# Thresholds of a top-64 attention by a sorting network in two of eight row blocks

## The reference, cut to what matters

```python
dots = jnp.einsum('hg,bgij->bhij', W_pre_th, dots)
dots = jnp.where(causal[None, None], mask_value, dots)
top = jax.lax.top_k(dots, TOPK)[0]          # TOPK = 64
vk = top[..., -1:]                          # the 64th largest: the row's threshold
dots = jnp.where(dots < vk, mask_value, dots)
attn = jax.nn.softmax(dots, axis=-1)
attn = jnp.einsum('hg,bgij->bhij', W_post_th, attn)
```

## Time and profile before

| what | value |
|---|---|
| three runs | 1380.62, 1382.27 (median), 1384.27 us |
| the profiled execution | 1383.52 us |
| its span | 1381.7 us, 18391 instructions |
| DVE busy | 1012.6 us, 73% of the span |
| PE busy | 932.9 us, 68% |
| ACT busy | 623.9 us, 45% |
| POOL busy | 131.1 us, 9% |
| mean granted TensorE clock | 0.785 of full speed |

### The profile page before, as it was taken

How to read it: one execution, slowest core, us unless ns; L and a number is a source line. 1 busy time by engine, 2 the same in 40 slices (tenths; PEclk the granted TensorE clock), 3 DMA queues, 4 the chain that set the end, 5 groups by cost and what they waited for, 6 DMA issues and landing times. The chain is left out here.

```text
span 1381.7 us, 18391 instructions
## 1 busy us (share of the span) xinstructions
PE 932.9 (68%) x6206; PEld 601.0 (43%) x6206; DVE 1012.6 (73%) x2568; ACT 623.9 (45%) x1349; POOL 131.1 (9%) x269
## 2 busy tenths in 40 slices
PE   5864766645886304245978748999887537868877
PEld 2532333322554104135965424666555224535644
DVE  5968998937564698986458666899787697957832
ACT  3746767641443405146125606556256303635622
POOL 0120000001000000000020120200201121120000
PEclk9975555556998656678999958999989758989967
DMA  5000000002355001011000000000000000000000
GB/s 201 1 1 0 1 1 1 1 0 92 83 116 128 20 0 64 6 58 61 4 1 1 1 1 0 1 1 1 1 1 2 0 0 1 1 1 1 2 0 15
DMA packets 26606, 30.11 MB, mean 22 GB/s; under 512 B 1169, under 2 KB 23057, under 8 KB 25490
## 3 DMA queue, kind: packets, MB, share of 16 engines
q1 hardware_dynamic: 26514, 28.95, 7.4%
HBM read 19.50 MB, written 9.44 MB: 21 GB/s over the span
## 5 line engine op out<-in xcount | busy, mean ns | idle before, releaser
L1845 DVE TENSOR_TENSOR_SCAN l2a_hs<-l2a_decay,l2a_b_ps 128x512 f32<-128x512 f32 x64 | 78.0, 1221 | 10.8 <-PE l2a_b_ps L1657 2.7
L1657 PEld LDWEIGHTS l2a_b_ps<-l2a_diag,l2a_uT 128*128 128x128 f32 x512 | 65.4, 195 | 36.3 <-issue 36.3
L1657 PE MATMUL l2a_b_ps<-l2a_diag,l2a_uT 128*128 128x128 f32 x512 | 70.6, 282 | 0.0
L2330 PE MATMUL l1w_mem_ps<-l1a_rows,l1w_post 128*128 128x64 f32 x16 | 4.6, 382 | 97.2 <-DVE l1a_rows L2472 97.2
L1665 PE MATMUL l2a_acc_ps<-l2a_hc,pack 128*128 128x512 f32 x128 | 65.7, 595 | 1.0 <-DVE l2a_hc L1854 1.0
L2445 DVE MATCH_REPLACE8 l1w_minus<-l1w_low,l1w_minus 128x129 f32<-128x129 f32 (+39 forms) x264 | 65.1, 296 | 0.0
L2358 ACT ACTIVATE l1w_score<-l1w_mix_ps 128x264 f32<-128x264 f32 (+7 forms) x29 | 12.0, 451 | 108.0 <-DVE l1a_rows L2472 92.3
L2439 DVE MAX8 l1w_low<-l1w_minus 128x8 f32<-128x129 f32 (+37 forms) x332 | 60.4, 289 | 0.4
L2320 PE MATMUL l1w_mix_ps<-l1a_rows,l1w_pre 128*128 128x264 f32 (+7 forms) x58 | 30.0, 687 | 42.3 <-DMA l1a_rows<-scores_dram 23.8
L1749 ACT ACTIVATE l2a_decay<-l2a_dt,pack 128x1016 f32<-128x1016 f32 x32 | 36.6, 1143 | 47.0 <-DVE l2a_hs L1845 47.0
L2330 PEld LDWEIGHTS l1w_mem_ps<-l1a_rows,l1w_post 128*128 128x128 f32 x16 | 4.0, 288 | 102.1 <-DVE l1a_rows L2472 100.9
(11 more groups left out here) (596 smaller groups left out, 2699.7 us busy)
## 6 DMA issues: line engine op xcount, KB each, us to landing
scores_dram<-l1p_dots SPq DMA_DIRECT2D x8, 924.0 KB, 7.1
l1a_rows<-scores_dram SPq DMA_DIRECT2D x5, 1056.0 KB, 4.7
l1a_rows<-scores_dram SPq DMA_DIRECT2D x24, 132.0 KB, 3.7
scores_dram<-l1p_dots SPq DMA_DIRECT2D x8, 132.0 KB, 3.5
pack<-in_pack SPq DMA_DIRECT2D x1, 761.5 KB, 9.5
pack<-in_pack SPq DMA_DIRECT2D x2, 321.5 KB, 6.9
pack<-in_pack SPq DMA_DIRECT2D x1, 612.0 KB, 11.5
pack<-in_pack SPq DMA_DIRECT2D x1, 576.0 KB, 10.5
```

The costliest lines, as they stand in the source:

```text
L1657: mm = nc.tensor.matmul(bx_ps(n)[:, j * S:(j + 1) * S], uT[:, c, b, :], diag[:, s % 2, b, :], start=True, stop=True)
L1845: nc.vector.tensor_tensor_scan(hs[:, n % 2, :], decay[:, k % 2, batches[half], :].rearrange("p b t -> p (b t)"), bx_ps(n), 0.0, ALU.mult, ...
```

## The change

Blocks 7 and 6 (`SORTED`) no longer search. Their negated rows lie in `neg`, a view of `minus` with a fixed pitch of J = 132 elements. In block 6 a memset fills columns 116 to 131 with the largest number. `sort` puts the first 64 and the second 64 elements of each of the 16 rows in ascending order by a bitonic network. Each step (`exchange`) is one `tensor_tensor` with min and one with max over 16 rows x 64 pairs. There are 1+2+3+4+5+6 = 21 steps. Every step reads one buffer and writes the other: `neg`, or `swap`, which is the space in `mixed` of queries 64 to 79, written by ACT only much later. In `swap` a following element of a row is 128 elements (512 bytes) further on. Each step waits for both instructions of the step before. After them one more min of the first half against the reversed second half leaves the 64 smallest of the 128 at columns 64 to 127; with the 4 columns behind them, 68 candidates, one MAX8 a row gives the threshold as the fifth largest (`at = MEM`). `maximum(n + 1)` is called after the first 10 steps. In the other three blocks with a threshold the search is as before, on the rows at a pitch of 132.

```diff
+SORTED = (7, 6)
+        neg = minus[:].rearrange("p (i j) -> p i j", j=J)
+        swap = mixed[:, :, S // 2:S // 2 + ROWS_K].rearrange("p e r -> p r e")
...
+                def exchange(low_out, high_out, a, b):
+                    after(dve, pair_set, pairs[0])
+                    nc.vector.tensor_tensor(low_out, a, b, ALU.min).then_inc(pair_set, 1)
+                    nc.vector.tensor_tensor(high_out, a, b, ALU.max).then_inc(pair_set, 1)
+                    pairs[0] += 2
+                def sort(w, between):
+                    if w < J:
+                        nc.vector.memset(neg[:, :, w:], -LOWEST).then_inc(pair_set, 1)
+                        pairs[0] += 1
+                    here, there = neg[:, :, 0:S], swap
+                    size = 2
+                    while size <= TOPK:
+                        groups = lambda z: z.rearrange("p r (g e) -> p r g e", e=size)
+                        lower = lambda z: groups(z)[:, :, :, 0:size // 2]
+                        mirror = lambda z: groups(z)[:, :, :, size // 2:][:, :, :, ::-1]
+                        exchange(lower(there), mirror(there), lower(here), mirror(here))
+                        here, there = there, here
+                        step = size // 4
+                        while step:
+                            near = lambda z: z.rearrange("p r (g e) -> p r g e", e=2 * step)[:, :, :, 0:step]
+                            far = lambda z: z.rearrange("p r (g e) -> p r g e", e=2 * step)[:, :, :, step:]
+                            exchange(near(there), far(there), near(here), far(here))
+                            here, there = there, here
+                            step //= 2
+                        if size == 16:
+                            between()
+                        size *= 2
+                    dve.wait_ge(pair_set, pairs[0])
+                    nc.vector.tensor_tensor(neg[:, :, TOPK:S], here[:, :, 0:TOPK], here[:, :, TOPK:S][:, :, ::-1],
+                                            ALU.min).then_inc(pair_set, 1)
...
-                        nc.vector.tensor_scalar(minus[:, a:ROWS_K * w], score[n % 2][:, a:ROWS_K * w], -1.0, None,
+                        nc.vector.tensor_scalar(neg[:, cut[0]:, 0:w], s[:, cut[0]:, :], -1.0, None,
...
+                        by_sort = k in SORTED
+                        if by_sort:
+                            sort(w, lambda: maximum(n + 1))
+                            for i in cut:
+                                nc.vector.max(low[:, i, :], neg[:, i, TOPK:J]).then_inc(kth, 1)
+                                n_kth += 1
-                        for r in range(max(keys[i] - TOPK for i in cut) // 8 + 1):
+                        for r in range(0 if by_sort else max(keys[i] - TOPK for i in cut) // 8 + 1):
...
-                            at = (keys[i] - TOPK) % 8
+                            at = MEM if by_sort else (keys[i] - TOPK) % 8
```

More of the change, by code:

```diff
@@ L2258, in mixed_weights @@
                  "exp_set", "minus_set", "kth", "taken", "bound_set", "kept", "recip_set", "weights_set", "at_mm", "at_set", "mem_mm",
-                 "mem_set", "mem_stored")
+                 "mem_set", "mem_stored", "pair_set")
         (pad_set, mats_set, mix_mm, mix_set, causal_set, max_set, neg_set, exp_set, minus_set, kth,
-         taken, bound_set, kept, recip_set, weights_set, at_mm, at_set, mem_mm, mem_set, mem_stored) = (sc.sem(n) for n in names)
+         taken, bound_set, kept, recip_set, weights_set, at_mm, at_set, mem_mm, mem_set, mem_stored, pair_set) = (sc.sem(n) for n in names)
         def block_of(buf, k):
@@ L2413, in maximum @@
                                             ALU.mult).then_inc(neg_set, 1)
+                pairs = [0]
+                def exchange(low_out, high_out, a, b):
[28 more added lines that the diff above has]
+                                            ALU.min).then_inc(pair_set, 1)
+                    pairs[0] += 1
+                    dve.wait_ge(pair_set, pairs[0])
                 maximum(0)
@@ L2421, in _ @@
                     if cut:
-                        a = cut[0] * w
                         if n_kth:
                             dve.wait_ge(kth, n_kth)
-                        nc.vector.tensor_scalar(minus[:, a:ROWS_K * w], score[n % 2][:, a:ROWS_K * w], -1.0, None,
+                        nc.vector.tensor_scalar(neg[:, cut[0]:, 0:w], s[:, cut[0]:, :], -1.0, None,
                                                 ALU.mult).then_inc(minus_set, 1)
@@ L2430, in _ @@
                         dve.wait_ge(minus_set, n_minus)
-                        neg = block_of(minus, k)
                         keys = {i: ROWS_K * k + i + 1 + MEM for i in cut}
-                        for r in range(max(keys[i] - TOPK for i in cut) // 8 + 1):
+                        by_sort = k in SORTED
[5 more added lines that the diff above has]
+                        for r in range(0 if by_sort else max(keys[i] - TOPK for i in cut) // 8 + 1):
                             for i in cut:
```

## The result

The changed kernel takes 1478.44 us (median of 4 runs, 1476.13 to 1480.54), the kernel before 1383.27 us (4 runs). The ratio is 1.0686, with a 95% interval of 1.0669 to 1.0703. It is slower by 95.2 us; the forecast was 1443 us, 60 us slower, with a range of 1394 to 1494.

What follows compares the result with a forecast made beforehand. DVE was taken to bound the kernel. Sort against search +15.5 us plus a layout surcharge of 45 us gave +60.5 us on 1383.5 us, 1444.0 profiled, stated as 1443 us against the median; range 1394 to 1494 us.

Steps and rivals of the forecast that it cites:

- rival 2: Sort's network in blocks 7 and 6: every stepped access pays, also writes; +107 us, 1489 us; chance 0.23.
- DVE is the bound, the whole difference reaches the end: Threshold stage: DVE busy 169.67 of 187.06 us, so its gain or loss moves the stage's end and the span.
- A step of the network 2.40 us: Blocks 7 and 6: one min and one max over 1024 f32 at 1.224 us each, with overlap and wait, 2.40 us.
- a sorted block 54.0 us: Blocks 7 and 6: 21 steps, the last min and sixteen MAX8 take 54.0 us on DVE without access surcharge.
- +15.5 us in all without the layout: Sort against search: block 7 -0.1 us, block 6 +15.6 us, together +15.5 us before any surcharge for stepped access.
- min and max cost what a subtraction costs: Network instructions: min and max take the duration of traced two-input operations, 1.224 us over 1024 f32.
- The sort costs the same for both blocks, the search doesn't: Blocks 7 and 6: 54.0 us sorted in each, while the search takes 54.11 us in 7 and 36.94 in 6.
- `maximum` moved at no cost: Row maxima called 24 us or more into the block: ACT's exponentials still end over 20 us early, so nothing.
- The layout: Accesses to `swap` at 512 bytes: surcharge 1.07 us on 21 instructions a block, 45 us taken, bounds 0 to 91.6.
- both inputs: Network instructions on `swap`: the surcharge, one more element time, falls only where both inputs of one operation are stepped.

Runs made afterwards that it cites:

- experiment 1: Changed kernel with the second buffer packed as 32 lists of 64 adjacent elements, both blocks sorted, against the kernel before: 1399.24 us, ratio 1.0101.
- the probe: Kernel before with extra single instructions put in ahead of the thresholds, each alone; min over 512 f32 took 0.69 us adjacent, 1.06 with one input at 16 bytes.

## Why the prediction was right or wrong

The measured time lies in the stated range only because the range took in rival 2, which had a chance of 0.23; the forecast itself was 35 us too low.

- *DVE is the bound, the whole difference reaches the end.* Right: 95.3 of 96.2 us lie in the two stretches.
- *A step of the network 2.40 us, a sorted block 54.0 us, and +15.5 us in all without the layout.* Right: 2.39 us, 53.9 us (54.53 less 0.6 for `maximum(1)`), +15.2 us as a kernel. Durations of a like operation from another stage, together with how far an instruction overlaps the next one and how long a dependent one waits, were enough to within a microsecond. That min and max cost what a subtraction costs, and reversal and short runs cost nothing, was right too.
- *The sort costs the same for both blocks, the search doesn't.* Right, and it is the design fault that remains when the layout is mended: 55.0 against 39.5 us in block 6.
- *`maximum` moved at no cost.* Right: what is left in experiment 1 is +15.2 us, where the sum without any cost for it was +15.5.
- *The layout: 1.07 us on each instruction with both inputs stepped, none on writes, 45 us.* This is the step that failed. Measured: 1.22 us on 42 reads (51.3 us) and 0.70 us on 44 writes (30.7 us), 82.0 us. With +15.5 that is 97.5 us, where the spans differ by 96.2; the 1.3 us between are not explained. The mechanism "both inputs" was wrong, and rival 2 (every stepped access pays; 1489 us) was the nearer case, with the price of a read 12% too low (1.07 for 1.22 us) and that of a write 53% too high (1.07 for 0.70).
- *Why I chose wrong.* I had three short rows. L1000 is a memset, and memsets paid nothing at any step that was tried: 0.48 us for 512 elements at 4, 16, 64 and 512 bytes alike. L1020 is a one-input operation over 16 elements, where the surcharge is too small to be seen: 174 ns stepped and 175 adjacent in the probe; over 512 elements it is 0.59 against 0.43 us. L1259 was the only row of the kind of operation that the change adds, and it showed the surcharge. But its output is stepped as well as its inputs, so it couldn't say which of them pays: over 8 elements the probe has 168 ns adjacent, 172 with both inputs at L1259's step and 174 with only the output at its step. The step "both inputs are needed" came from the other two rows, which are of other operations. That 7 ns over 8 elements came near the price of a long read (1.07 us for 1.22) was in part luck: the long operations paid about 0.7 ns an element at 32 bytes and 1.2 at 512, and L1259 could not know of the second.

The Trainium skill's note in "SBUF — State Buffer", section "Door 1: The DMA port swizzle", predicted a cost for all 43 instructions. These runs agree that fewer than two elements to 16 bytes are dear and that reads and writes both pay (from 0.69 to 1.06 us over 512 elements). The note also puts the stride that is free at 4 f32 elements; here 4 paid in full and 3 in part (0.83 us), and the measurement decides.

## What to carry to other kernels

Before elements of a tile are laid apart on VectorE, look at the step that each instruction makes: at 16 bytes or more a two-input f32 operation took 1.5 to 1.7 times as long here, and nearly twice where both inputs stepped by 512 bytes and started a multiple of 256 bytes apart. A network over fixed sizes has a cost that does not shrink with the data, so compare it with the search block by block; here it tied on 117 to 132 keys and lost 15 us on 101 to 116, and no version run here beats the kernel before. And when a short row is used as evidence on a price for each element, it has to be of the same kind of operation, and long enough: a min over 8 elements with one input at 16 or 516 bytes took 166 to 168 ns, as an adjacent one does (168), and only over 32 elements was there a clear difference (208 to 210 against 193).

## What the runs showed of the hardware that was not expected

- ScalarE pays more than VectorE: a copy of 512 f32 within SBUF took 0.631 us adjacent, 1.107 us read at 16 bytes and 1.063 us written at 512 bytes. That is 0.43 to 0.48 us more, against 0.33 to 0.38 for a VectorE min and 0.16 to 0.20 for a one-input VectorE operation.
- GpSimd paid for stepped reads and not for the one stepped write that was tried: an addition over 512 f32 took 1.264 us adjacent, 2.105 us with both inputs at 16 bytes, and 1.274 us with the output at 512 bytes.
- A one-input VectorE operation took 0.43 us adjacent and 0.59 to 0.63 us at steps from 16 to 512 bytes, for input or output. A reduction took 0.69 us adjacent and 1.05 with its input at 16 bytes.
